# A two-layer correlation kernel: the order of the first units' steps, the tiles that GpSimd makes, and the waits inside the products

## The reference

```python
x = x + conv_ref(gn(x), w0, b0)      # gn: 32 groups of 16 channels
x = x + conv_ref(gn(x), w1, b1)

def conv_ref(feature, conv_w, conv_b):
    norm = sqrt(sum(feature * feature, axis=channels))
    fn = feature / max(norm, 1e-12)
    fp = pad(fn, 2 on each side)
    sims = [sum(fp[:, :, r:h+r, cc:w+cc] * fn, axis=channels) for cc in range(5) for r in range(5)]
    x = concatenate([feature, stack(sims)], axis=channels)      # 512 + 25 rows
    return relu(einsum('bihw,oi->bohw', x, conv_w) + conv_b)
```

## Time and profile before

| | |
|---|---|
| median of 3 runs | 490.61 us (490.59 to 491.08) |
| the profiled execution | 490.72 us, span 489.0 us |
| TensorE matmuls busy | 436.7 us (89% of the span) |
| VectorE busy | 367.2 us (75%) |
| ScalarE busy | 291.6 us (60%) |
| GpSimd busy | 111.2 us (23%) |
| mean granted TensorE clock | 0.986 of full |

### The profile page before, as it was taken

One profiled execution on the slowest core, in us unless ns is written; L12 is line 12 of the kernel. 1 busy time (PEld: TensorE's weight loads), 2 busy tenths in 40 slices (PEclk: granted clock), 3 DMA queues, 4 the chain that ended last, 5 costly groups with the idle time before them and its releaser, 6 DMA issues.

```text
span 489.0 us, 13950 instructions
## 1 busy us (share of the span) xinstructions
PE 436.7 (89%) x5896; PEld 222.6 (46%) x5896; DVE 367.2 (75%) x871; ACT 291.6 (60%) x349; POOL 111.2 (23%) x168
## 2 busy tenths in 40 slices
PE   0368599677989999999998999999999999999996
PEld 0334245332445445454544455554545454544442
DVE  6899788768969798879878797979888787424322
ACT  1754474839388575949385767767584939513231
POOL 4421401031311404031312304040403131223100
PEclk9989899989999999999999999999999999999999
DMA  7662543132320555368666764040313143545322
GB/s 293 271 192 72 150 159 88 47 75 61 91 64 23 152 173 168 101 222 251 205 190 232 220 230 129 24 124 29 101 40 96 50 149 90 172 155 179 120 118 86
DMA packets 33989, 65.88 MB, mean 135 GB/s; under 512 B 11756, under 2 KB 21028, under 8 KB 33926
## 3 DMA queue, kind: packets, MB, share of 16 engines
q1 hardware_dynamic: 24014, 55.95, 34.7%
q0 software_dynamic: 9792, 8.92, 7.5%
q10 hardware_dynamic: 120, 0.11, 0.1%
HBM read 33.54 MB, written 28.87 MB: 128 GB/s over the span
## 4 chain that ended last, share of the span: by engine, by line
PE 57%; DVE 21%; ACT 7%; DMA 6%; issue 5%; POOL 2%; SPq 1%; ACTq 0%; DVEq 0%
PE conv_ps L611 45%; DVE stats L866 6%; PE conv_ps L620 4%; DVE operands L914 4%; PE gram_ps L533 4%; ACT v L731 3%; DMA vol<-corr_h 2%; DVE xs L999 2%; ACT operands L723 2%; PE gram_ps L546 2%; DMA rn_far<-rows_dram 1%; DVE operands L920 1%; DMA skew<-band_dram 1%; DVE wl L987 1%; ACT act_out L760 1%
## 5 line engine op out<-in xcount | busy, mean ns | idle before, releaser
L611 PE MATMUL conv_ps<-operands,wh 128*128 128x512 f16 x1024 | 329.1, 384 | 6.6 <-ACT act_out L760 4.3
L611 PE MATMUL conv_ps<-operands,wl 128*128 128x512 f16 x512 | 196.0, 383 | 0.0
L611 PEld LDWEIGHTS conv_ps<-operands,wh 128*128 128x128 f16 x1024 | 101.6, 99 | 127.6 <-ACT act_out L760 6.5
L760 ACT ACTIVATE act_out<-conv_ps,bias,wdown 128x512 f32<-128x512 f32 x128 | 95.4, 772 | 88.3 <-PE conv_ps L620 85.9
L999 DVE TENSOR_TENSOR xs<-xs,act_out 128x512 f32<-128x512 f32 x128 | 85.9, 685 | 37.7 <-ACT act_out L760 37.7
L723 ACT ACTIVATE operands<-xs,affine 128x1024 f16<-128x1024 f32 x64 | 93.1, 1462 | 17.5 <-DVE affine L906 17.5
L914 DVE TENSOR_TENSOR operands<-v,operands 128x1024 f16<-128x1024 f32 x64 | 79.3, 1240 | 27.2 <-ACT v L731 23.1
L866 DVE BATCH_NORM_STATS2 stats<-xs 128x6 f32<-128x512 f32 x128 | 79.9, 684 | 2.4 <-DMA xs<-in_x_dram 2.4
L611 PEld LDWEIGHTS conv_ps<-operands,wl 128*128 128x128 f16 x512 | 50.5, 99 | 56.1 <-issue 2.4
L731 ACT ACTIVATE v<-xs,affine 128x1024 f32<-128x1024 f32 x55 | 72.6, 1319 | 0.4 <-DVE operands L914 0.4
L533 PE MATMUL gram_ps<-operands 128*32 128x108 f16 (+1 forms) x2048 | 49.2, 215 | 15.0 <-DVE operands L920 9.8
(11 more groups left out here) (75 smaller groups left out, 221.0 us busy)
## 6 DMA issues: line engine op xcount, KB each, us to landing
xs<-in_x_dram SPq DMA_DIRECT2D x32, 512.0 KB, 7.4
out_dram<-xs SPq DMA_DIRECT2D x32, 512.0 KB, 3.0
band_dram<-band SPq DMA_DIRECT2D x64, 120.0 KB, 2.3
skew<-band_dram SPq DMA_DIRECT2D x32, 222.5 KB, 3.0
vol<-corr_h POOLq DMA_DIRECT2D x48, 50.0 KB, 3.1
rows_dram<-rows SPq DMA_DIRECT2D x32, 65.8 KB
rows_dram<-rows SPq DMA_DIRECT2D x32, 63.3 KB
mirror<-rows_dram POOLq DMA_DIRECT2D x14, 110.9 KB, 2.5
```

The source lines that it names most:

```text
L611: pe.matmul(conv_ps[:, g % 4, :], w[:, l, t, m * P:(m + 1) * P], opnd[:, u % RING, part, t, n * HALF:(n + 1) * HALF], start=(t == 0 and w ...
L760: act.activation(in_rows(act_out[:, g % AOUT, :]), by_rows(conv_ps[:, g % 4, :]), ACT.Relu, bias=bias[:, l, m:m + 1], scale=wdown[:, l, m: ...
```

## The change

- VectorE: `unit_affine(1)` and `neighbours(0)` come ahead of all five `low_weights(0, n)`; before, four of these stood ahead of the affine and the fifth behind the first tile of unit 1. `correlation(0)` comes ahead of the fourth statistics tile of unit 2.
- TensorE: `turn(0)` and then both of `channels(0, 0)` and `(0, 1)` wait for all five low weights; the products of unit 1 are made in one go, tile by tile over both banks, between `channels(0, 1)` and `channels(0, 2)`. `average(4)` comes behind `products(3, 1)`.
- `products(u, n)` waits in front of each tile: for unit 3 for that tile's low and halved part, for the others for all four, four times.
- Unit 3's exact tiles 1 and 3 are made by GpSimd, behind `volume_in(1)`. In ScalarE's queue `rectified(1, 1)` comes behind `exact_tile(3, 2)`.

```diff
-        ON_POOL = {0: (0, 1, 2), 1: (0, 1, 2), 2: (0, 1, 2)}
+        ON_POOL = {0: (0, 1, 2), 1: (0, 1, 2), 2: (0, 1, 2), 3: (1, 3)}
@@ gpsimd
             volume_in(pool, 1)
+            exact_tiles(3, pool_tiles(3))
@@ tensor
-            def first_products():
+            def products_by_tile(u):
                 pe.wait_ge(gram_clear, 1)
+                wait(pe, band_sb, BANKS * u)
                 for t in range(KT):
-                    pe.wait_ge(low, t + 1)
-                    pe.wait_ge(halved, t + 1)
+                    pe.wait_ge(low, KT * u + t + 1)
+                    pe.wait_ge(halved, KT * u + t + 1)
                     for n in range(BANKS):
-                        last = bank_products(0, n, t)
+                        last = bank_products(u, n, t)
                         if t == KT - 1:
                             last.then_inc(gram, 1)
             def products(u, n):
-                pe.wait_ge(low, KT * (u + 1))
-                pe.wait_ge(halved, KT * (u + 1))
                 pe.wait_ge(band_sb, BANKS * (u - 1) + n + 1)
                 for t in range(KT):
+                    pe.wait_ge(low, KT * u + (t if u == STEADY else KT - 1) + 1)
+                    pe.wait_ge(halved, KT * u + (t if u == STEADY else KT - 1) + 1)
                     last = bank_products(u, n, t)
                 last.then_inc(gram, 1)
@@ tensor, the start
-            first_products()
+            products_by_tile(0)
             for n in range(KT + 1):
                 turn_weights(0, n)
             average(1)
-            pe.wait_ge(w_low, KT)
+            turn(0)
+            pe.wait_ge(w_low, W_LOWS)
             channels(0, 0)
-            turn(0)
             channels(0, 1)
+            products_by_tile(1)
             channels(0, 2)
-            pe.wait_ge(w_low, W_LOWS)
-            products(1, 0)
             channels(0, 3)
-            products(1, 1)
             average(2)
@@ tensor, the loop
                     if k == STEADY and j == LED:
+                        products(k, 1)
                         average(k + 1)
-                        products(k, 1)
@@ scalar
             exact_tile(3, 0)
             norm_tile(3, 1)
             rectified(1, 0)
-            exact_tile(3, 1)
             norm_tile(3, 2)
-            rectified(1, 1)
             lengths(2)
             exact_tile(3, 2)
+            rectified(1, 1)
             norm_tile(3, 3)
-            exact_tile(3, 3)
             rectified(1, 2)
@@ vector
-            for n in range(KT):
-                low_weights(0, n)
             unit_affine(1)
             neighbours(0)
-            low_tile(1, 0)
-            half_tile(1, 0)
-            low_weights(0, KT)
-            for t in range(1, KT):
+            for n in range(KT + 1):
+                low_weights(0, n)
+            for t in range(KT):
                 low_tile(1, t)
                 half_tile(1, t)
-            for t in range(KT):
+            for t in range(KT - 1):
                 stats_tile(2, t)
+            correlation(0)
+            stats_tile(2, KT - 1)
             stats_done(2)
-            correlation(0)
```

## The result

The changed kernel takes 494.88 us (median of 10 runs, 492.41 to 496.45) where the kernel before takes 490.68 (10 runs, 488.15 to 493.82): a ratio of 1.0082 [1.0053, 1.0111]. It is 0.8% slower; forecast was 0.45% faster, and 494.88 lies above the range of 486.0 to 491.6. The profiled execution of the changed kernel took 492.44 us (span 490.7), near the low end of its runs, and the trace explains that execution: 1.7 us over the profiled one of before. What stands between 492.4 and the median is taken up at the end. In this document a ratio leaves out executions in the program's slower state, so it can differ a little from the quotient of the medians beside it.

What follows compares the result with a forecast made beforehand. TensorE is full from 140 us, so the start's VectorE and ScalarE chain decides. 2.15 us lost by unit 3's affine, more won behind it: unit 4's average copy 2.1 earlier, plus 0.2; 490.72 - 2.3 = 488.4 us, range 486.0 to 491.6.

Steps and rivals of the forecast that it cites:

- low clock for TensorE's first groups: At `channels(0, 0)`, in the start: 1.6 us more for the lower clock behind the long pause.
- A: End of unit 3's affine on VectorE; forecast at 83.9 against 81.77 before, so 2.15 us lost.
- third rival: Unit 3: GpSimd's tiles block VectorE for their whole length, leaving nothing of 1.35 us won; 489.9 us, chance 0.12.
- slower rival: Later `products` calls: added wait borders cost 0.06 us each, 72 of them 4.3 us; 492.7 us, chance 0.12.
- So `average(2)` at 54.6: TensorE in the start: from 39.5, four `channels` 10.4, lower clock 1.6, unit 1's products 3.1 us.
- second rival: Pause without visible cause in `products_by_tile(1)` or unit 3: 2.2 us more, 490.6 us, chance 0.16.
- the copy: Copy of unit 4's average, the prediction's measure: forecast 102.1 against 104.19; later than 104 would show it wrong.
- clock rival: TensorE's clock stays up at `channels(0, 4)`: 1.6 us less, 486.8 us, chance 0.20.
- The other half of the sum: Unit 3, from A to the copy: forecast 18.2 us, after GpSimd's two tiles win 1.35 us at the last half tile.
- credit for the vanished pause of 2.37 us: `products(3, 0)`: forecast running tile by tile behind `turn(2)` to A + 13.3, then `channels(1, 6)` at the full clock.

Runs made afterwards that it cites:

- waits_only: Kernel before, with the waits on low and halved in front of each of the four tiles in every `products` call, nothing else; 490.04 us, ratio 0.999.
- old_vector_order: Changed kernel with VectorE's order of before (four low weights, then unit 1's affine and neighbours), TensorE's order as changed; 494.0 us, ratio 1.0077.
- start_only: Kernel before with only the change's new order of the start on VectorE and TensorE; 494.63 us, ratio 1.0103.
- average_early: Changed kernel with `average(2)` ahead of `channels(0, 3)` instead of behind it; 489.49 us, ratio 0.9991.
- after_again: Changed kernel run once more with no edit, for a second profile; 491.77 us, ratio 1.0049.
- unit3_only: Kernel before with GpSimd making unit 3's exact tiles 1 and 3, ScalarE's order for them, and unit 3's products waiting by tile; 486.66 us, ratio 0.994.

## Why the prediction was wrong

**What held.** Low weights at 39.6 (forecast 39.5), unit 1's tiles 46.7 (46.5), `correlation(0)` 50.27 (50.1), statistics of unit 2 at 54.38 (54.1). The low clock for TensorE's first groups was as charged. GpSimd's third tile of unit 1 held VectorE up by 1.12 us (1.1 charged):

```profile
40.93 2.72 POOL L476 TENSOR_SCALAR v<-xs,affine 128x1024 f32<-128x1024 f32 x1 [6.06 <-DVE operands L912]
...
43.75 1.23 DVE L912 TENSOR_TENSOR operands<-v,operands 128x1024 f16<-128x1024 f32 x1 [1.12 <-POOL v L476]
```

Unit 3's last `half_tile` ended 12.2 us behind A (12.05), so GpSimd's tiles held VectorE up no longer than was charged (third rival). The slower rival, the waits, fell: products of a later unit still take 1.4 us (the row below, changed kernel; forecast's own row is the earlier trace rows), and `waits_only` has 0.999 [0.9957, 1.0023].

```profile
188.00:192.00 4.00, 1.44 (x64) 1.29 (x64) 1.00 0.81 267
```

**What failed.** The step "So `average(2)` at 54.6". Its sum took `products_by_tile(1)` for "twice 1.43 with a border", 3.1 us. It took 5.3, from 46.38 to 51.71, because of the pause of 2.47; the two groups behind it took the 5.2 that were charged. The prediction had this case as its second rival, "a pause without a visible cause again", with a chance of 0.16; the argument against it was that eight other groups of products ran through. Those were runs of at most 128. In the runs of 256 that the change makes, the pause came in all six profiles (2.47, 1.74, 1.67, 1.95, 2.18, 1.75). So it should have been a term of the sum. The rival's price of 2.2 us was too low as well, for a second step hangs on it: `channels(0, 4)` could start 2.2 later than forecast (61.59 against 59.4) behind 3.33 us of idleness in one piece, where the forecast had 1.3 and 2.3 with a microsecond of work between, and it cost 2.4 us at the low clock, not 1.7. By A the loss was 5.2 and not 2.15, 3.1 more than forecast; from A to the copy another 0.5 (18.67 against 18.2). 102.1 + 3.1 + 0.5 = 105.7, which is the row, and a copy later than 104 is what the prediction named as a sign of being wrong.

The clock rival, "the clock stays up", did not happen in either profile of the changed kernel, but in `old_vector_order` it stayed up behind 3.41 us of idleness, while `channels(0, 4)` of `start_only` ran at 0.50 behind 2.71. The length of the idle time just before a group alone doesn't decide it; what does, no run here told.

**The other half of the sum** was right in its mechanism: from A to the copy it had 4.2 us won (22.4 to 18.2), the profile shows 3.8, and unit 3's part alone is worth 3.1 us, 0.6%, as a median. The credit for the vanished pause of 2.37 us was due: no kernel with the waits by tile in unit 3 has it. The prediction gave no reason why it should vanish, so that part was luck. But what the change removed there it made anew in unit 1, at a place with more behind it.

**What stays open.** The changed kernel's profiled execution is 2.4 us under its median, and two sets of runs have medians of 494.88 and 491.77. The profile of the second set, 491.57, is like its median, and both profiles show the same start (copy at 105.68 and 105.35), so nothing in the start that a profile shows accounts for it. The start as profiled puts the copy 3.6 us later than forecast, and the profiled execution ended 4.0 later; the rest of the 6.5 us between 488.4 and 494.88 has no row. One candidate shows in the traces. Near 400 us some profiles have a stand for nothing visible: 1.74 in the changed kernel, 1.74 in `average_early`, 3.27 in `old_vector_order`. All three come behind the same 5268 matmul records, and TensorE goes on 2.2 to 2.4 us after a packet of instructions started, as in the start. The changed kernel:

```profile
402.20 0.39 PE L613 MATMUL conv_ps<-operands,wh 128*128 128x512 f16 x1 [1.74 <-issue]
```

`after_again`, the same program, has no pause there, and its packet started some 130 matmuls sooner. So the place is fixed, but not whether the pause comes, and executions of one program can differ by it. None of the six profiles with before's waits in the later units has it; how much of the medians it makes isn't shown. Nor is it shown why the parts sum to +0.33% when the whole has +0.5 to +0.8%.

**The best version.** `unit3_only`, 486.66 us, and with `average(4)` moved as well, 486.73, against 489.81 and 490.03 of before beside them: the change's unit 3 without its start. `split_early`, the whole change with unit 1's products split and `average(2)` ahead of `channels(0, 3)`, has 487.76; its start brings nothing that `unit3_only` lacks.

## What to carry to other kernels

When an edit joins two runs of small matmuls into one, charge it a pause of some 2 us, and look for how the kernel's own rows of idleness "for nothing" lie in its instruction stream: they come back at a place, not by chance. A small matmul on which the next unit hangs (here an average of 0.3 us) goes ahead of a group as soon as its input is there; one group of 2.6 us in front of it went with 4.8 us at the next unit's affine in the pair of profiles here (part of it the clock), and 2.3 us or more in the medians. Time parts of a change apart before judging it: this one held a gain of 0.6% and a loss of 1.0%.

## What the hardware showed that was not expected

- TensorE stands 1.7 to 2.5 us in a run of 256 small matmuls (weights of 32 columns), in six of six profiles, at the same matmul counted from the start of the program; in two runs of 128 with a group of twelve 512-column matmuls between them, none in the same place. A run of 128 is no protection by itself: `products(3, 0)` of before stands 2.37 and 2.17 us, both times after 121.
- The granted clock of `channels(0, 4)` behind 3.3 to 3.4 us of idleness was 0.54 once and 1.00 once (stretch 61 to 67 us of the changed kernel and of `old_vector_order`).
- In `waits_only`, 84 more borders with two waits each that are already met, between matmuls that follow one another every 11 ns (128 in 1.4 us), cost nothing that can be measured: ratio 0.999 [0.9957, 1.0023]. In the changed kernel the products' 64 matmuls of one line take 1.44 us, before 1.43.
- GpSimd's exact tiles of unit 3 took 2.70 us, beside VectorE's back-to-back two-input steps, and 1.38 us. GpSimd waits for VectorE as VectorE does for GpSimd. The changed kernel's timeline of GpSimd:

```profile
87.12 2.70 POOL L476 TENSOR_SCALAR v<-xs,affine 128x1024 f32<-128x1024 f32 x1 [0.47 <-DVE affine L904]
...
92.64 1.38 POOL L476 TENSOR_SCALAR v<-xs,affine 128x1024 f32<-128x1024 f32 x1 [2.82 <-DVE operands L912]
```
